# A graph network's second dense stage stores y as rows, and its last dense stage normalises rows on VectorE

## The reference, cut to what matters

```
h = relu(layernorm(x) ...)                      # h: result of the layers before
x_r = h @ Wskip + bskip                         # second attention layer, nodes without edges: y = sigmoid(gate) * x_r
h = relu(gamma * (y - mean) * rsqrt(var + EPS) + beta) + h_res      # batch norm over all nodes
x1 = x + h
n = relu(layernorm(x1))
out = x1 + relu(concat([n, agg, u]) @ W2a + b2a) @ W2b + b2b
```

## Time and profile before

| | us |
|---|---|
| median of three runs | 2683.86 (2680.4 to 2684.52) |
| the profiled execution, its own time | 2679.54 |
| its span, first to last instruction | 2677.8 |

### The profile page before, as it was taken

The page is one execution under the profiler, slowest core; times in us unless marked ns, Lnnn a source line. Parts: engine busy times, 40 slices in busy tenths (PEclk is TensorE's granted clock), DMA queues, the critical chain, the costliest instruction groups (busy, mean ns, idle before and its releaser), DMA issues. The chain is left out here.

```text
span 2677.8 us, 38819 instructions
## 1 busy us (share of the span) xinstructions
PE 2133.3 (80%) x7614; PEld 1191.9 (45%) x7614; DVE 1708.6 (64%) x4970; ACT 1374.2 (51%) x2609; POOL 1293.6 (48%) x1119
## 2 busy tenths in 40 slices
PE   1888888897879656788848879569999989399997
PEld 0444444442223233344423323247677767166665
DVE  3888888872169778677751179657777776355552
ACT  1777877781112144566622222147676765366662
POOL 4444444417730000445448700067777764567774
PEclk9988899997779878899978889769999999699998
DMA  4676777753323287899953313399999996344440
GB/s 136 210 235 225 222 225 224 227 194 105 91 57 93 72 288 256 321 369 371 383 165 85 81 43 91 94 263 298 301 294 303 296 302 190 106 103 112 113 116 22
DMA packets 309081, 514.10 MB, mean 192 GB/s; under 512 B 86165, under 2 KB 182100, under 8 KB 308827
## 3 DMA queue, kind: packets, MB, share of 16 engines
q1 hardware_dynamic: 259000, 479.60, 56.5%
q0 software_dynamic: 46400, 33.03, 5.9%
q10 hardware_dynamic: 3552, 0.13, 0.1%
HBM read 291.41 MB, written 221.80 MB: 192 GB/s over the span
## 5 line engine op out<-in xcount | busy, mean ns | idle before, releaser
L474 POOL DMA_INDIRECT first_x<-in_x,first_index x200 | 256.3, 1281 | 296.1 <-issue 286.7
L741 POOL DMA_INDIRECT second_entry<-node_map,second_si x100 | 135.2, 1352 | 289.5 <-issue 184.6
L338 ACT ACTIVATE first_xn<-first_x,first_nb,first_rstd 125x128 f32<-125x128 f32 x600 | 245.1, 485 | 35.0 <-DVE first_nb L518 35.0
L994 PE MATMUL last_psH<-last_g,W2a 128*128 128x500 f32 x400 | 200.0, 625 | 35.3 <-DVE last_hid L956 35.1
L576 PE MATMUL first_psZ<-first_h,gate_h 128*128 128x500 f32 x250 | 141.3, 649 | 82.1 <-DVE first_y L537 82.0
L1268 DVE SCALAR_TENSOR_TENSOR att_prod<-att_bank,bk,att_qs 128x500 f32<-128x500 f32 x50 | 37.0, 739 | 253.4 <-ACT att_qs L1235 253.4
L1003 PE MATMUL last_psO<-W2b,last_hid 128*125 128x128 f32 x1600 | 192.3, 274 | 0.0
L1027 POOL DMA_INDIRECT elast_x<-x_rows,elast_si x100 | 140.3, 1404 | 95.6 <-issue 86.0
L1003 PEld LDWEIGHTS last_psO<-W2b,last_hid 128*125 128x125 f32 x1600 | 184.2, 189 | 0.9 <-issue 0.9
L660 POOL TENSOR_TENSOR bn_rs<-bn_rs,power 128x1 f32<-128x1 f32 x2 | 1.2, 580 | 348.1 <-DVE bn_rs L650 348.1
L338 ACT ACTIVATE last_xn<-last_x,last_nb,last_rstd 125x128 f32<-125x128 f32 x400 | 164.0, 487 | 0.1
(11 more groups left out here) (261 smaller groups left out, 5353.0 us busy)
## 6 DMA issues: line engine op xcount, KB each, us to landing
hT<-first_h SPq DMA_DIRECT2D x100, 250.0 KB
yT<-first_y SPq DMA_DIRECT2D x100, 250.0 KB, 3.8
second_yin<-yT SPq DMA_DIRECT2D x50, 500.0 KB
second_hin<-hT SPq DMA_DIRECT2D x50, 500.0 KB
yT<-second_y SPq DMA_DIRECT2D x50, 500.0 KB
last_yin<-yT SPq DMA_DIRECT2D x50, 500.0 KB
first_x<-in_x SPq DMA_DIRECT2D x100, 224.0 KB
h_rows<-second_rows SPq DMA_DIRECT2D x50, 448.0 KB
```

The costliest lines, as they stand in the source:

```text
L338: last = act.activation(xn[:, j], x[:, j], ACT.Relu, bias=nb[:, j:j + 1], scale=rstd[:, j:j + 1])
L474: pool.indirect_dma_start(x[:, to % X, j], None, a["x"], bass.IndirectOffsetOnAxis(index[:, end, r % 2, j:j + 1], 0), bounds_check=NODES - ...
L741: pool.indirect_dma_start(entry[:, q], None, scratch.node_map, bass.IndirectOffsetOnAxis(si[:, q], 0), bounds_check=NODES - 1, oob_is_err= ...
L994: last = pe.matmul(psH[h][:, 0:CH], w.W2a[:, 0, h * 128:(h + 1) * 128], g[:, q % 2], start=True, stop=True)
```

## The change

The second stage turns `y` into rows with four more TensorE transposes a chunk (`turn_y`, bank `psY`) and ScalarE copies them out (`make_yrows`); the pair is stored as rows, one pipeline step later, in two transfers. The rows of `h2` and of `y` have one PSUM bank each, where `h2` had two. `y` has four buffers where it had eight.

The last stage loads `y` as rows. The batch norm's scale and shift stand on the partitions; before the loop two VectorE products with the identity, one TensorE product with ones and a copy spread them over rows (`bn_row`). In the loop VectorE multiplies and adds with `bn_row` broadcast over the four tiles (`scale`), and `make_x1` takes the relu and adds `xh` in one instruction. ScalarE's `bn` and TensorE's `turn` are gone from the loop. The second half of the MLP relu moves from VectorE to ScalarE (`make_hid1`). The edge chunks keep their column path.

```
+def over_tiles(row):
+
+    return row.rearrange("p (o f) -> p o f", o=1).to_broadcast([TILE, TILES, D])
...
-        y = ph.sb("y", [128, U, CH])
-        psR = [ph.ps(f"psR{s}") for s in range(2)]
+        y = ph.sb("y", [128, 4, CH])
+        yrows = ph.sb("yrows", [TILE, U, TILES, D])
+        psR, psY = ph.ps("psR"), ph.ps("psY")
...
                 def store_y(t, q, r):
-                    hold(sp, ph.seen, m.y, made(2 * t + 1))
-                    sp.dma_start(cols_of(scratch.yT, t * 2 * CH, 2 * CH), pair_cols(y, q)).then_inc(y_stored[q], 16)
-
-                pipeline(sp, NCHUNK // 2, U // 2, [(0, load), (5, store_rows), (6, store_y)])
+                    hold(sp, ph.seen, m.yrows, made(2 * t + 1))
+                    dst = pair_rows(scratch.y_rows, t * 2 * CH)
+                    sp.dma_start(dst[0:SPLIT], pair(yrows, q)[0:SPLIT]).then_inc(y_stored[q], 16)
+                    sp.dma_start(dst[SPLIT:TILE], pair(yrows, q)[SPLIT:TILE]).then_inc(y_stored2[q], 16)
+
+                pipeline(sp, NCHUNK // 2, U // 2, [(0, load), (5, store_rows), (7, store_y)])
...
-                    act.copy(flat(rows, q), psR[q % 2][0:TILE]).then_inc(m.rows, 1)
+                    act.copy(flat(rows, q), psR[0:TILE]).then_inc(m.rows, 1)
+
+                def make_yrows(k, q, r):
+                    act.wait_ge(m.y_turned, made(k))
+                    act.wait_ge(y_stored[q // 2], 16 * r + 16)
+                    act.wait_ge(y_stored2[q // 2], 16 * r + 16)
+                    act.copy(flat(yrows, q), psY[0:TILE]).then_inc(m.yrows, 1)
...
-                pipeline(act, NCHUNK, U, [(3, make_sig), (0, bn), (3, make_rows)])
+                pipeline(act, NCHUNK, U, [(3, make_sig), (0, bn), (3, make_rows), (6, make_yrows)])
...
-                    dve.wait_ge(m.ystats, made(k - U))
-                    dve.wait_ge(y_stored[q // 2], 16 * r + 16)
-                    dve.scalar_tensor_tensor(out=y[:, q], in0=psX[q % 2][:, 0:CH], scalar=w.bskip[:, 1:2],
+                    dve.wait_ge(m.ystats, made(k - 4))
+                    dve.wait_ge(m.y_turned, made(k - 4))
+                    dve.scalar_tensor_tensor(out=y[:, q % 4], in0=psX[q % 2][:, 0:CH], scalar=w.bskip[:, 1:2],
...
-                    pe.wait_ge(m.rows, made(k - 2))
-                    to_rows(pe, psR[q % 2], h2[:, q], w.ident, False, m.turned)
+                    pe.wait_ge(m.rows, made(k - 1))
+                    to_rows(pe, psR, h2[:, q], w.ident, False, m.turned)
+
+                def turn_y(k, q, r):
+                    pe.wait_ge(m.y, made(k))
+                    pe.wait_ge(m.yrows, made(k - 1))
+                    to_rows(pe, psY, y[:, q % 4], w.ident, False, m.y_turned)
...
-                pipeline(pe, NCHUNK, U, [(2, skip), (2, turn)])
+                pipeline(pe, NCHUNK, U, [(2, skip), (2, turn), (5, turn_y)])
...
-        yin = ph.sb("yin", [128, U, CH])
-        hin, xin = (ph.sb(n, [TILE, U, TILES, D]) for n in ("hin", "xin"))
+        yin, hin, xin = (ph.sb(n, [TILE, U, TILES, D]) for n in ("yin", "hin", "xin"))
+        diag, bn_row = ph.sb("diag", [128, 2, D]), ph.sb("bn_row", [TILE, 2, D])
         xh = ph.sb("xh", [TILE, 4, TILES, D])
-        act1 = ph.sb("act1", [128, 2, CH])
+        z = ph.sb("z", [TILE, 2, TILES, D])
...
-        psR = [ph.ps(f"psR{s}") for s in range(2)]
+        psB = ph.ps("psB")
...
                 def load(t, q, r):
-                    hold(sp, ph.seen, m.bn, made(2 * t + 1 - U))
-                    sp.dma_start(pair_cols(yin, q), cols_of(scratch.yT, t * 2 * CH, 2 * CH)).then_inc(y_loaded[q], 16)
+                    hold(sp, ph.seen, m.scaled, made(2 * t + 1 - U))
+                    move_rows(sp, pair(yin, q), pair_rows(scratch.y_rows, t * 2 * CH), y_loaded[q])
...
-                def bn(k, q, r):
-                    act.wait_ge(y_loaded[q // 2], 16 * r + 16)
-                    act.wait_ge(m.turned, made(k - 2))
-                    act.activation(act1[:, q % 2], yin[:, q], ACT.Relu, bias=w.bn[:, 1:2], scale=w.bn[:, 0:1]).then_inc(m.bn, 1)
...
+                def make_hid1(k, q, r):
+                    act.activation(hid[:, q % 4, 1], psH[1][:, 0:CH], ACT.Relu, bias=w.b2u[:, 1:2]).then_inc(m.hid1, 1)
...
-                pipeline(act, NCHUNK, U, [(9, make_hid0), (7, make_g), (5, make_xn), (0, bn), (3, edges(edges_bn))])
+                pipeline(act, NCHUNK, U, [(9, make_hid0), (9, make_hid1), (7, make_g), (5, make_xn), (3, edges(edges_bn))])
...
+                def scale(k, q, r):
+
+                    dve.wait_ge(y_loaded[q // 2], 32 * r + 32)
+                    dve.wait_ge(m.x1, made(k - 2))
+                    dve.tensor_tensor(z[:, q % 2], yin[:, q], over_tiles(bn_row[:, 0]), ALU.mult).then_inc(m.scaled, 1)
+                    dve.wait_ge(m.scaled, made(k))
+                    dve.tensor_tensor(z[:, q % 2], z[:, q % 2], over_tiles(bn_row[:, 1]), ALU.add).then_inc(m.shifted, 1)
+
                 def make_x1(k, q, r):
-                    dve.wait_ge(m.turned, made(k))
+                    dve.wait_ge(m.shifted, made(k))
                     dve.wait_ge(m.xh, made(k))
                     dve.wait_ge(x1_stored[q // 2], 16 * r + 16)
                     dve.wait_ge(x1_stored2[q // 2], 16 * r + 16)
                     dve.wait_ge(m.x1b, made(k - 8))
-                    dve.tensor_tensor(flat(x1, q), psR[q % 2][0:TILE], flat(xh, q % 4), ALU.add).then_inc(m.x1, 1)
+                    dve.scalar_tensor_tensor(out=flat(x1, q), in0=flat(z, q % 2), scalar=0.0, in1=flat(xh, q % 4),
+                                             op0=ALU.max, op1=ALU.add).then_inc(m.x1, 1)
...
-                def make_hid1(k, q, r):
-                    dve.wait_ge(m.hidden, made(k))
-                    dve.wait_ge(m.o_ps, made(k - 4))
-                    dve.tensor_scalar(hid[:, q % 4, 1], psH[1][:, 0:CH], w.b2u[:, 1:2], 0.0, ALU.add, ALU.max).then_inc(m.hid1, 1)
...
-                pipeline(dve, NCHUNK, U, [(4, edges(edges_h3)), (6, edges(edges_rows)), (9, make_hid1), (4, bias), (2, make_x1), (11, make_o), (2, stats), (2, aggr)])
+                dve.tensor_scalar(diag[:, 0], w.ident[:], w.bn[:, 0:1], None, ALU.mult)
+                dve.tensor_scalar(diag[:, 1], w.ident[:], w.bn[:, 1:2], None, ALU.mult).then_inc(bn_row_step, 1)
+                dve.wait_ge(bn_row_step, 2)
+                dve.tensor_copy(bn_row[:].rearrange("p t f -> p (t f)"), psB[0:TILE, 0:2 * D]).then_inc(bn_row_step, 1)
+                dve.wait_ge(bn_row_step, 3)
+                pipeline(dve, NCHUNK, U, [(4, edges(edges_h3)), (6, edges(edges_rows)), (4, bias), (1, scale), (2, make_x1), (11, make_o), (2, stats), (2, aggr)])
...
-                def turn(k, q, r):
-                    pe.wait_ge(m.bn, made(k))
-                    pe.wait_ge(m.x1, made(k - 2))
-                    to_rows(pe, psR[q % 2], act1[:, q % 2], w.ident, False, m.turned)
+                pe.wait_ge(bn_row_step, 1)
+                pe.matmul(psB[0:TILE, 0:2 * D], w.ones[:, 0:TILE], diag[:].rearrange("p t f -> p (t f)"), start=True, stop=True).then_inc(bn_row_step, 1)
...
-                pipeline(pe, NCHUNK, U, [(5, edges(turn_edges)), (1, turn), (8, hidden), (6, turn_back), (10, output)])
+                pipeline(pe, NCHUNK, U, [(5, edges(turn_edges)), (8, hidden), (6, turn_back), (10, output)])
```

More of the change, by code:

```diff
@@ L176, in prepare @@
         w2u = ph.sb("w2u", [128, 256])
-        ones = ph.sb("ones", [128, D])
+        ones = w.ones
         win = ph.sb("win", [ECHUNK, CH + 2], I32)
@@ L678, in dense_second @@
         y_loaded, h_loaded = ph.loaded("y_loaded", U // 2), ph.loaded("h_loaded", U // 2)
-        rows_stored, rows_stored2, y_stored = (ph.stored(n, U // 2) for n in ("rows_stored", "rows_stored2", "y_stored"))
+        rows_stored, rows_stored2, y_stored, y_stored2 = (ph.stored(n, U // 2) for n in ("rows_stored", "rows_stored2", "y_stored", "y_stored2"))
         src, src_row = ph.sb("src", [TILE, NCHUNK], I32), ph.sb("src_row", [TILE, NCHUNK], I32)
@@ L682, in dense_second @@
         src_loaded, src_stored, looked_up = ph.count("src_loaded"), ph.count("src_stored"), ph.loaded("looked_up", U)
-        m = Group(**{n: ph.stage(n + "_made") for n in "si row bn h2 turned rows xz sig y ystats".split()})
+        m = Group(**{n: ph.stage(n + "_made") for n in "si row bn h2 turned rows xz sig y ystats y_turned yrows".split()})
         with nc.Block() as block:
@@ L710, in _ @@
                 sp.wait_ge(src_stored, 16)
-                for sems in (rows_stored, rows_stored2, y_stored):
+                for sems in (rows_stored, rows_stored2, y_stored, y_stored2):
                     for q in range(U // 2):
@@ L770, in ystats @@
                     dve.wait_ge(m.y, made(k))
-                    dve.bn_stats(w.ystats[:, bass.ds(k * 6, 6)], y[:, q]).then_inc(m.ystats, 1)
+                    dve.bn_stats(w.ystats[:, bass.ds(k * 6, 6)], y[:, q % 4]).then_inc(m.ystats, 1)
                 dve.wait_ge(src_loaded, 16)
@@ L819, in dense_last @@
```

(7 more changed lines are left out.)

## The result

The changed kernel takes 2700.74 us (median of 8 runs, 2692.96 to 2705.83) against 2683.02 for the kernel before (8 runs, 2676.65 to 2692.97). The ratio is 1.0075, 95% interval 1.0058 to 1.0092: slower by some 18 to 20 us, where 2716 was forecast with 2650 to 2775 as range. The profiled execution took 2705.83 us, its span 2704.1.

The account below looks back on a forecast made before the run. The prediction took DMA transfers as the bound, TensorE next. Row loads 18, exclusion 8, row store 4 and drain 4 made 34 us on 2679.5, 2713.5; with the median 4.3 us above that execution it forecast 2716, range 2650 to 2775.

Parts of the forecast that it names:

- Its own signs: Observations named beforehand as showing the forecast right or wrong: DMA share, GB/s, chunk time, engine shares, instruction times, second-stage length.
- the last stage at 297 GB/s: Last stage: a rate of 297 GB/s or more would show the forecast wrong; falling below 297 would show it right.
- Bound of both stages: Second and last dense stages: DMA transfers set the pace, TensorE is next, about 0.5 us a chunk behind in the last.
- The rival with TensorE as the bound: Last stage: TensorE sets the pace, so losing its turn gives back 44 us; about 2648, faster; chance 0.2.
- Row loads in the last stage, 18 us: Last stage: loading y as rows instead of columns costs 18 us, between bounds of 0 and 47.
- the upper bound: Last stage: if row loads cause all the loss from 411 to 272 GB/s, loading y as rows costs 47 us.
- Exclusion, 8 us: Last stage: VectorE instructions with two SBUF inputs and GpSimd adds exclude each other; 8 us not hidden by transfers' slack.
- The sum of 493 us of exclusive work: Last stage: mutually exclusive VectorE and GpSimd instructions total 493 us in about 510, fitting with nothing to spare.
- The first rival: Last stage: exclusion sets the pace, a GpSimd add slipping in between VectorE's instructions every chunk, 5.6 us; about 2760; chance 0.2.
- Second stage's row store, 4 us out of bounds 0 to 30: Second stage: storing y as rows costs 4 us, as the mixed stage runs near the rate of pure column loads.
- TensorE and ScalarE in the second stage hidden: Second stage: TensorE's four added transposes (43 us) and ScalarE's added copy (57 us) fit under the transfers.
- Drain, 4 us: End of the second stage: turn, copy and later store lengthen the drain by 4 us.

Follow-up runs that it names:

- e2: The old second stage with the new last stage, which loads h2 rows in place of y: 2684.99 us against 2682.05 for the kernel before, ratio 1.0005.
- n1: The kernel before without the last stage's load of x, GpSimd adding h2 to itself: 2611.76 us against 2683.87 for the kernel before, ratio 0.9742.
- s1: Changed kernel, y rows in an own table with 4,096-byte pieces, transfers still cut into 112 and 13 partitions: 2696.36 us against 2680.01 for the kernel before.
- p1: Changed kernel with 4,096-byte pieces in all row transfers of the last stage: 2705.80 us against 2683.87 for the kernel before, ratio 1.0090.
- s2: Changed kernel, y rows in an own padded table, one store and one load a pair over 128 partitions: 2682.37 us against 2683.87 for the kernel before.
- n2: The changed kernel without the last stage's load of x, GpSimd adding h2 to itself: 2640.45 us, ratio 0.9844 to the kernel before.
- e4: Kernel before, the second stage storing h2 rows again in row shape instead of y's columns: 2697.03 us against 2682.05 for the kernel before, ratio 1.0043.
- c1: Kernel before with the second stage's column store of y cut into 112 and 16 partitions: 2698.18 us against 2680.01 for the kernel before, ratio 1.0068.
- e3: Old last stage; second stage turns y and copies rows out but stores columns as before: 2679.43 us against 2682.05 for the kernel before, ratio 0.9993.
- c3: Kernel before, column store of a pair as two one-chunk transfers over 128 partitions, 2,000-byte pieces: 2685.39 us against 2680.01 for the kernel before, ratio 1.0015.

## Why the prediction was right, and where its terms were off

The forecast (slower, transfers as the bound) holds, and its 32 us are 1.6 to 1.8 times the measured ones. That the total came so near is partly luck: two errors of opposite sign made it up. Of its 34 us, 26 stood in the last stage, where e2 leaves 7.5 at most, and 8 in the second, where the profiled execution has 18.6 (14.3 and 4.3). Its own signs say the same. TensorE under 90% in the last stage came (88%), and so did medians near 0.7 us with maxima near 2 for the multiply and the add (at most 1.77). But the last stage at 297 GB/s was among the signs of being wrong, from chunk to chunk it is 5.11 us and not 5.3, and the second stage is 18.6 us longer, not at most 10.

- Bound of both stages: right. n1 shows it for the last stage: a sixth of the bytes gone, 72 us gone, and TensorE next at 4.42 us a chunk, where 4.30 and some 0.2 were read from the earlier trace rows. The rival with TensorE as the bound falls with it.
- Row loads in the last stage, 18 us: mis-sized, about 0 over the stage. The rate in its steady part is 297 GB/s with the column load and with the row loads. The step that failed is the reasoning of the upper bound: the 272 GB/s of the opening were laid on row loads all through the stage, but four of its five node transfers were cut at 112 already, and cutting the fifth made no difference behind the opening. The opening itself did get slower, 241 GB/s over 22 us, and its first `o` 6.9 us later. In e2, s1 and p1 it is as late (62.8 to 63.4 us behind the first load; 55.0 to 58.5 with the old form) and in s2, which loads over 128 partitions, 59.8; these four win it back in the loop (474.7 to 484.1 us from first to last `o`, where the old form has 485.9 to 494.7); by what, is not shown.
- Exclusion, 8 us: GpSimd and VectorE do wait for each other, and the cost is hidden. VectorE was forecast at 447 us of 520 and took 450.6; GpSimd went from 369.9 to 447.8 by waiting, nearly all of it in `ve` and `rstd`. The sum of 493 us of exclusive work had left these two out, 21 and 102 us before. With them it would be 616 in a stage of about 510, which could not fit at 6.2 us a chunk, and yet a chunk takes 5.11: they wait for a running VectorE instruction but don't hold up the next one. The floor that the new work makes is 4.53 us a chunk in n2 and 4.76 with the full add, 0.11 and 0.34 over TensorE's 4.42, and both are under 5.04. The first rival is excluded: its 5.6 us was a wait for every chunk.
- Second stage's row store, 4 us out of bounds 0 to 30: mis-sized, this is the largest term. The loop grew by 14.3 us, and the store alone makes it (e4, c1, s2). It was sized by the mixed stage being near the rate of pure column loads; but there one transfer in four was cut, and now it is two in four.
- TensorE and ScalarE in the second stage hidden: right (e3). Drain, 4 us: right, 4.3.
- The Trainium skill, "SBUF — State Buffer", says what the prediction drew on in the section behind "Door 1: The DMA port swizzle", "Can I just issue two DMAs to hit both halves?": only one transfer over all 128 partitions reaches all the ports. The trace agrees in the second stage that 128 partitions are better, 372 GB/s with them (s2) against 348 with the same pieces cut (s1). Two transfers in place of one cost little when each has all 128 (c3, 364 GB/s), and that ports are the reason is shown by no run. The forecast had weighed the rule against the last stage's load, where it changed nothing outside the opening, and not against the second stage's store, where it was 14 us.
- The Trainium skill's section "Who interferes with whom" agrees where GpSimd comes second, 1.02 to 1.46 us for one `rstd`. The other way round it depends on the instruction: VectorE's waited for an `x1b` (1.65 us instead of 0.69) and not for an `rstd` (0.69).

Open: why a cut transfer costs the second stage 14 us and not the last. e2's interval would hide up to 7.5 us. Which of the sixteen DMA engines carries which partitions was not looked at.

No version beat the kernel before. s2 equals it: it keeps the row form and pays nothing for it that shows.

## What to carry to other kernels

Where transfers set the pace, compare each moved transfer's partitions and cuts as well as its bytes: in the second stage one transfer of 112 partitions and a remainder in place of 128 cost 5 to 7% of the rate (353 for 373 GB/s, 348 for 372), with the same pieces; in the last stage it cost nothing that shows. An intermediate table that no one indexes by row can have any layout, so it can be padded to 128 partitions. To learn whether added compute is hidden, take a transfer away on both sides and compare the floors, and see that this leaves the compute as it was: here it made GpSimd's add 0.23 us cheaper. A forecast whose total comes true should still be held against its own signs, stage by stage.

## What the runs showed of the hardware

- A store cut into 112 and 16 partitions slowed the second stage from 373 to 353 GB/s between 1100 and 1350 us although bytes and pieces are the same (c1); two stores over 128 partitions with pieces half as long gave 364 (c3).
- A VectorE instruction with both inputs in SBUF makes a GpSimd instruction that starts inside it wait, even one on 125 x 4 numbers: `rstd` 1.02 us alone, 1.41 to 1.47 in all 55 cases between 1820 and 2150 us. A large GpSimd add holds up such a VectorE instruction too (1.65 us instead of 0.69), the small `rstd` doesn't (0.69 with `rstd` under way).
- A GpSimd add of 125 x 512 numbers takes 1.04 us when both inputs are the same tile and 1.27 when they are two (n2 and the changed kernel, medians).
- TensorE's granted clock between 1820 and 2150 us, a mean of its two levels (1.2 GHz stands as 0.5, 2.4 GHz as 1.00), was 0.96 before, 0.92 after, and 1.00 in n1 and n2. In the changed kernel it was 1.00 from 1832 to 1836 us, while TensorE worked 1.69 of 4 us, then 0.60 from 1836 to 1840 and 0.97 from 1840 to 1844. No run here prices it.
